# A graph layer's merged output phase: one group of edge sums per head-group step, in place of 2, 1, 1, 0, 0, 1

## The reference

```python
def _gat_layer(x, src, dst, W, a_src, a_dst, bias, concat):
    h = (x @ W).reshape(N, H, C)
    al_s = jnp.einsum('nhc,hc->nh', h, a_src)
    al_d = jnp.einsum('nhc,hc->nh', h, a_dst)
    e = jax.nn.leaky_relu(al_s[src] + al_d[dst], NEG_SLOPE)
    m = jax.ops.segment_max(e, dst, num_segments=N)
    ex = jnp.exp(e - m[dst])
    denom = jax.ops.segment_sum(ex, dst, num_segments=N)
    alpha = ex / (denom[dst] + 1e-16)
    msg = h[src] * alpha[:, :, None]
    out = jax.ops.segment_sum(msg, dst, num_segments=N)
...
    k_sum = jnp.sum(k_prime, axis=-2)
    d_inv = 1.0 / jnp.einsum('bhnm,bhm->bhn', q_prime, k_sum)
    context = jnp.einsum('bhnm,bhnd->bhmd', k_prime, v)
    out = jnp.einsum('bhnm,bhmd,bhn->bhnd', q_prime, context, d_inv)
    out = out.transpose(0, 2, 1, 3).reshape(B, N, C)
    return out @ w_proj.T + b_proj
...
    x = x + _L0_gnn_ref(...) + _L0_mix_ref(...)
```

## Time and profile before

| | us |
|---|---|
| median of 3 runs | 4442.09 (4439.57 to 4449.44) |
| the profiled execution, its own time | 4442.09 |
| its span in the trace | 4439.7 |
| the merged phase, from the second `edge_turn` to the last (23 tiles) | 731.5 |
| the same for one tile | 31.8 |

### The profile page before, as it was taken

The page is one execution under the profiler, slowest core; times in us unless marked ns, Lnnn a source line. Parts: engine busy times, 40 slices in busy tenths (PEclk is TensorE's granted clock), DMA queues, the critical chain, the costliest instruction groups (busy, mean ns, idle before and its releaser), DMA issues. The chain is left out here.

```text
span 4439.7 us, 67390 instructions
## 1 busy us (share of the span) xinstructions
PE 3819.4 (86%) x23483; PEld 3098.0 (70%) x23484; DVE 2147.0 (48%) x4835; ACT 1170.3 (26%) x2391; POOL 1363.7 (31%) x1368
## 2 busy tenths in 40 slices
PE   6774988988898949999699976888888579999998
PEld 5773666666666628888699974555555379999997
DVE  6753555555555634444322213655555444445444
ACT  1222323333333323333211112222222222222222
POOL 1123555555555500000000005666666211111110
PEclk8897999999999969999899987999999789999999
DMA  5765766666766533333466637888888410000000
GB/s 202 254 242 196 221 201 201 220 199 200 219 200 200 183 132 129 131 142 128 131 77 79 78 89 276 310 315 313 317 314 303 166 57 22 21 24 26 21 21 14
DMA packets 239565, 729.54 MB, mean 164 GB/s; under 512 B 75503, under 2 KB 80650, under 8 KB 230995
## 3 DMA queue, kind: packets, MB, share of 16 engines
q1 hardware_dynamic: 151315, 351.47, 26.0%
q0 software_dynamic: 88000, 374.95, 25.8%
HBM read 642.07 MB, written 145.41 MB: 177 GB/s over the span
## 5 line engine op out<-in xcount | busy, mean ns | idle before, releaser
L873 POOL DMA_INDIRECT k_rows<-tab,k_pick x576 | 593.0, 1030 | 494.8 <-PE k_num L1293 346.8
L1996 POOL DMA_INDIRECT m_rows<-tab,m_e x500 | 500.6, 1001 | 271.5 <-issue 144.8
L1293 PE MATMUL k_num<-k_rows,k_wt 128*64 128x384 f32 (+1 forms) x2400 | 450.9, 528 | 32.2 <-ACT k_wt L960 32.1
L1293 PEld LDWEIGHTS k_num<-k_rows,k_wt 128*64 128x64 f32 x2400 | 175.3, 147 | 258.8 <-issue 213.8
L133 PE MATMUL g_prod<-g_w_hi,g_h_h 128*128 128x384 f32 x800 | 269.5, 337 | 1.5 <-DVE g_h_l L1594 1.5
L135 PE MATMUL g_prod<-g_w_hi,g_h_l 128*128 128x384 f32 x800 | 267.5, 334 | 0.0
L134 PE MATMUL g_prod<-g_w_lo,g_h_h 128*128 128x384 f32 x800 | 267.3, 334 | 0.0
L133 PE MATMUL f_prod<-f_w_hi,f_a_h 128*128 128x512 f32 x600 | 243.9, 407 | 0.0
L2289 PE MATMUL m_out<-m_rows,m_wt 128*32 128x384 f32 x2000 | 207.7, 548 | 35.4 <-ACT m_wt L2045 35.4
L1455 DVE TENSOR_TENSOR f_a_l<-f_turn,f_a_h 128x384 fp32r<-128x384 f32 x200 | 110.6, 553 | 260.2 <-ACT f_a_h L1431 259.7
L135 PE MATMUL f_prod<-f_w_hi,f_a_l 128*128 128x512 f32 x600 | 235.5, 393 | 0.0
(11 more groups left out here) (292 smaller groups left out, 8871.4 us busy)
## 6 DMA issues: line engine op xcount, KB each, us to landing
agg<-k_outb SPq DMA_DIRECT2D x100, 384.0 KB, 4.6
f_a_in<-agg SPq DMA_DIRECT2D x100, 384.0 KB
h<-f_e SPq DMA_DIRECT2D x25, 1024.0 KB, 4.1
g_h<-h SPq DMA_DIRECT2D x25, 1024.0 KB, 12.8
tab<-q_xn SPq DMA_DIRECT2D x25, 388.5 KB, 6.5
tab<-g_row SPq DMA_DIRECT2D x25, 385.5 KB, 4.9
m_own<-tab SPq DMA_DIRECT2D x25, 385.5 KB
q_x<-in_x SPq DMA_DIRECT2D x25, 384.0 KB, 6.1
```

The lines of the kernel that those rows point to most:

```text
L873: pool.indirect_dma_start(rows[:, place(u, n), :], None, dram["tab1"], at, bounds_check=bound, oob_is_err=False).then_inc(rows_in[i], 16)
L1293: mm = pe.matmul(num[i][64 * g:64 * g + 64, 0:n], wt[:, 2 * c + g, :], rows[:, place(u, 2 * c + g), a:a + n], start=(c == 0), stop=(c == 2 ...
L1996: pool.indirect_dma_start(rows[:, place(h, c) + k, :], None, tab, bass.IndirectOffsetOnAxis(ap=e[h % 4][:, 0, k * SLOTS + c:k * SLOTS + c ...
```

## The change

The table goes, and step g does group g: one group in each of the steps 0 to 4, none in step 5. So group 0 stays in step 0, group 1 moves from step 0 to 1, group 2 from 1 to 2, group 3 from 2 to 3 (behind `project`), and group 4 from step 5 to step 4 (right behind `edge_turn`). No instruction is added or dropped, and no other engine's list is touched.

```diff
@@ -1857,7 +1857,6 @@
     XR = 5
     HALF = ((0, 384), (384, D + 1 - 384))
-    SUMMED = ((0, 1), (2,), (3,), (), (), (4,))
     tab = dram["tab2"]
@@ -2310,9 +2309,8 @@
                         if merged and t < NT and g == 4:
                             edge_turn(t)
-                        if merged and t >= 1:
-                            for c in SUMMED[g]:
-                                edge_sums(t - 1, c)
+                        if merged and t >= 1 and g < SLOTS:
+                            edge_sums(t - 1, g)
                     if merged and t < NT:
                         edge_spread(t)
```

## The result

The changed kernel takes 4491.85 us (median of 4 runs, 4488.94 to 4496.94), the kernel before 4440.83 us beside it. The ratio is 1.0113, 95% interval 1.0096 to 1.0131: 51 us slower. The forecast was slower by 18.8 us, the range ended at 4479. Direction and place were right, the size was not.

The account below looks back on a forecast made before the run. PE was taken to set the pace in the merged phase. 24 x 1.5 - 24.1 = 11.9 us for the chain plus 6.9 for the clock made 18.8 on 4442.1, so 4461 us; range 4444 to 4479.

Parts of the forecast that it names:

- longer tile at full clock, all tiles: Merged phase: each tile 1.03 us longer, from DVE held up 1.5 us less 0.47 us of group-4 wait; 24.7 us in all.
- cost of half clock in the phase: Merged phase: low clock costs 20.8 us before; the forecast's change in it, restated afterwards, is -5.9 us.
- The bound and the chain: Merged phase: PE sets the pace; `turns(t, 5)`, DVE's move to shift, ACT's exponential, then group 0, 1.03 us later a tile.
- the clock's part: Eleven tiles with clock falls behind `edge_turn`: slowed group 4 and transposes add 2.4 and 4.5 us, together 6.9.
- eight at 0.3, three at 1.5: Falls behind `edge_turn`: eight tiles slow only part of the transposes, 2.4 us; three slow group 4 and transposes, 4.5 us.
- the long waits for group 4: DVE's waits ahead of `sums`: eight of 1.43 to 1.59 us, three of 1.82 to 2.09, within the 24.1 us credited.
- the upper end: Merged phase: every tile pays 1.03 us (24.7) and has a low-clock stretch of 1.4 us (12.8 more): +38 us.
- Rival A: Behind the wait at `edge_turn`: group 4's matmuls keep PE's clock up, +3 to +9 us, about 4448; chance 0.12.
- The groups 1 to 3: Steps 1 to 3: moving these groups a step later causes no new wait on PE; cost 0.
- The rivals: Clock stays up, chance 0.12; no change, 0.06; faster because gathers were the bound, 0.10; much slower through late gathers, 0.04.
- The logits' line: DVE's idle ahead of the logits' first use of gathered rows: 0.4 us over all tiles, cited against gathers being the bound.
- POOL's wait: POOL's waits for the sums (m_out), 119.8 us before, were to shrink without any effect.

Follow-up runs that it names:

- half rows: Kernels before and changed with gathers fetching 384 numbers a row in place of 771, output not the layer's: 4642.7 and 4644.5 us.
- zero weights: Kernels before and changed with the edge weights set to zero, output not the layer's: 4653.4 and 4652.2 us.
- the shifted kernel: Changed kernel with groups 0, 1, 2 in steps 1, 2, 3 and groups 3, 4 in step 4 ahead of `edge_turn`: 4608.6 us, ratio 0.9919.

## Why the prediction was wrong

The 51.3 us between the two spans come apart so, with the forecast in the same terms:

| term | forecast | measured |
|---|---|---|
| longer tile at full clock, all tiles | 24 x 1.03 = 24.7 | 23 x (32.06 - 30.90) = 26.7 |
| cost of half clock in the phase | 18.8 - 24.7 = -5.9 | (775.8 - 23 x 32.06) - 20.8 = 17.6 |
| ahead of the first tile with sums | 0 | 2727.2 - 2720.1 = 7.1 |
| sum | 18.8 | 51.4 |

The last tenth of a us is what the phases and tiles outside of these terms differ by.

*The bound and the chain* were right. PE sets the pace on the first chip, DVE had no slack at the move of step 5, and 1.02 us a tile is what group 4 ahead of the transposes costs at full clock (8.36 against 7.34). It was forecast as 1.03, and came again as a difference of medians with half rows and zero weights (8.37 against 7.35), where the means differ by only 0.6. The other 0.14 us a tile stand behind group 0.

*The step that failed* is the clock's part, with the bound drawn from it: forecast at -5.9 us in the terms above, measured at +17.6. I took the falls of the old order as given and asked what each would cost at its old place: eight at 0.3, three at 1.5. I even credited the long waits for group 4 (24.1 - 24 x 0.47 = 12.8 us) to the new order, although they came from those falls. And the upper end had at most one fall a tile at 1.4 us. The changed order has two falls in most tiles, and such a tile costs 34.04 - 32.06 = 2.0 us more. Most of this is the first fall's: four tiles with that one alone, 0.8 to 1.0 us behind `edge_turn`, take 33.2 to 33.5 us. Both of the forecast's reasons for a small cost were turned round: the first fall slows group 4 and the transposes, which now come one after the other in front of DVE's chain, and the new wait brings a second fall. Rival A named this risk in one sentence and the range did not follow it. At 24 x 2.0 for the falls less 20.8, the upper end would have been 24.7 + 27.2 = 52. (The range was also written 1 us too low at both ends: 4442.1 + 3 and + 38 are 4445 and 4480.)

The Trainium skill (TensorE: Matmul & The Clock Gate, A second HAM failure mode: psum-queue depth-cycling) has frequent short idling between groups of matmuls as a cause of such swings. The trace of the changed kernel agrees so far as a granted clock of 0.54 and 0.50 stands behind waits of 1.9 and 1.2 us; that the waits are the cause no run here shows.

*Why the falls come in each tile* is read from two traces and not shown by an experiment. In the kernel before tiles of 30.9, 32.0 and 32.6 us alternate; in the changed one thirteen of 23 lie within 0.2 us of each other, so that each tile meets the fall at the same place. I take this for a coincidence of lengths, which I could not have read from the old trace; no run tests it. Nor is it shown that it hangs on group 4 alone: with groups 1 to 3 alone, on the later chips, the median time to group 0 was 8.4 to 8.8 us in place of 7.35, with the spread 4.0 to 4.4 us after `edge_turn` (2.97 before), and I had expected no effect there at all. The whole clock's part rests on the one pair of traces of the first chip.

*7.1 us* arose in phases that the change does not touch (the ends of the last three ahead of it are later by 3.9, 5.0 and 7.0 us in turn). The kernel before itself ran from 4437 to 4449 us, so this part need not come from the change.

*The groups 1 to 3* were costed at nothing. The first chip's traces have them at 0.14 us a tile at full clock at most. On the other chips they alone are worth 59 and 72 us, and 37 with half rows, by fewer tiles in which PE is held back: with them alone moved, 4 or 5 of 23 tiles stay below 25.5 us behind group 0, with the other orders one at most, but for the shifted kernel.

*The rivals.* None came: not A either, since the clock fell more often and not less. The logits' line has 0.5 us idle over all tiles in the changed kernel. POOL's wait grew from 119.8 to 178.9 us, not the shrinking that I had expected: with the sums spread, it stands for long twice a tile. No cost of it shows at the logits.

*Left open:* whether the falls lock to the tile whenever this order runs at the first chip's pace, what holds PE back at granted clock 1.00 in the later runs, why groups 1 to 3 help there, and why the changed kernel's gain of 0.7% was absent with half rows and with zero weights.

## What to carry to other kernels

When work moves in front of an instruction that another engine waits for, price it by that engine's slack at that place; for a tile at full clock this gave the chain's 1.0 us to within a few hundredths. Do not credit a wait of the old trace that came from a fall of the clock, and let the range hold a fall behind each wait of each turn of the loop, at what the slowed work costs on the chain. Do not carry a verdict of 1% on an order of instructions to another chip or another hour: the same two kernels were 1.1% apart one way in the first pair of runs and 0.7% the other way on a later chip.

## What the runs showed of the hardware

PE can be slowed without a sign in the granted clock. On six chips, in most tiles and mostly 7 to 12 us after PE resumed with group 0, sets of weight loads went from 0.32 to about 1.4 us apart for some 6 us at a granted clock of 1.00, and in most of these tiles the clock fell to half after it. It stayed with the DMA engines at 0.49 and with zero edge weights, and was absent in all 23 tiles of both traces of the first chip. The shifted kernel, on one of the six, shows half clock in its place (0.81 in the mean).
